# Toeplitz matrices of a long convolution: 64 rows fetched and 64 copied, or 32 rows fetched and 96 copied

## What is computed

```python
K  = _dplr_kernel(...)                                   # 64 channels x 1101 taps
Kf = jnp.fft.rfft(K, n=2 * L, axis=-1)
uf = jnp.fft.rfft(x, n=2 * L, axis=1)                    # x: (8, 1101, 64), normalized tokens
h1 = jnp.fft.irfft(uf * Kf.T[None], n=2 * L, axis=1)[:, :L, :]   # causal convolution
y1 = gelu(h1 + D * x)
y2 = gelu(y1 @ W_fc.T + b_fc) + x
y  = layernorm(y2) * ln_g + ln_b
```

## Time and profile before

| | us |
|---|---|
| median of 3 runs | 1528.23 |
| lowest and highest | 1527.93, 1532.77 |
| profiled execution | 1524.09 |
| its span, first to last instruction | 1522.4 |
| convolution loops on PE, first to last matmul | 202.1 to 299.3 |
| busy: PE, DVE, ACT, POOL | 1217.3, 827.2, 831.6, 427.0 |
| mean granted TensorE clock | 0.918 of full speed |

### The profile page before, as it was taken

How to read it: one execution, slowest core, us unless ns; L and a number is a source line. 1 busy time by engine, 2 the same in 40 slices (tenths; PEclk the granted TensorE clock), 3 DMA queues, 4 the chain that set the end, 5 groups by cost and what they waited for, 6 DMA issues and landing times.

```text
span 1522.4 us, 28792 instructions
## 1 busy us (share of the span) xinstructions
PE 1217.3 (80%) x11006; PEld 613.6 (40%) x11103; DVE 827.2 (54%) x1688; ACT 831.6 (55%) x1050; POOL 427.0 (28%) x624
## 2 busy tenths in 40 slices
PE   4894558880579988998998898899989889989942
PEld 3462357760235433433443343343344334334321
DVE  4844873357653645474575456457546554833443
ACT  0231134440245776587587667758857766876810
POOL 2000040026532123324242432423333243242321
PEclk9996779995579999999999999999999999999965
DMA  9999179704092055028008403701820560290000
GB/s 155 186 170 186 24 161 206 158 1 101 24 151 28 13 113 86 1 70 138 12 13 140 66 13 83 123 2 34 147 39 13 110 96 1 73 137 2 4 13 10
DMA packets 122173, 117.99 MB, mean 78 GB/s; under 512 B 74621, under 2 KB 91276, under 8 KB 121882
## 3 DMA queue, kind: packets, MB, share of 16 engines
q1 hardware_dynamic: 117988, 115.60, 41.8%
q10 hardware_dynamic: 3733, 0.60, 0.3%
q0 software_dynamic: 320, 0.04, 0.0%
HBM read 88.36 MB, written 22.95 MB: 73 GB/s over the span
## 4 chain that ended last, share of the span: by engine, by line
PE 38%; DVE 10%; ACT 8%; POOL 6%; issue 6%; DMA 5%; SPq 3%; POOLq 0%; DVEq 0%; ACTq 0%
PE b_pso L1974 12%; PE b_pss L1950 10%; ACT b_pb L2084 6%; POOL b_stat L2109 4%; DMA qk_parts_b<-b_qs 3%; PE b_psm L2031 3%; PE b_psm L2001 3%; DMA b_qop<-bound_part 2%; PE b_psm L2017 2%; PE b_psm L1933 2%; POOL b_pb L2128 1%; PE b_psm L2010 1%; PE b_psm L2036 1%; PE b_psm L2013 1%; SPq L1885 1%
## 5 line engine op out<-in xcount | busy, mean ns | idle before, releaser
L2084 ACT ACTIVATE b_pb<-b_pss 128x1024 f32<-128x1024 f32 (+2 forms) x736 | 661.2, 934 | 301.1 <-PE b_pss L1950 222.1
L2128 POOL TENSOR_SCALAR_AFFINE_SELECT b_pb<-b_pb 128x256 f32<-128x256 f32 (+1 forms) x544 | 224.5, 431 | 675.1 <-ACT b_pb L2084 668.8
L1974 PE MATMUL b_pso<-b_pb,b_vop 128*32 128x77 f32 (+4 forms) x5376 | 374.5, 385 | 35.2 <-POOL b_pb L2128 32.7
L1950 PE MATMUL b_pss<-b_qop,b_kop 128*128 128x512 bf16 (+3 forms) x1439 | 322.9, 331 | 32.7 <-DMA b_qop<-bound_part 12.4
L1950 PEld LDWEIGHTS b_pss<-b_qop,b_kop 128*128 128x128 bf16 x1536 | 125.7, 101 | 212.2 <-ACT b_pb L2084 96.7
L1974 PEld LDWEIGHTS b_pso<-b_pb,b_vop 128*32 128x32 f32 x5376 | 112.8, 109 | 210.8 <-issue 164.6
L2320 DVE TENSOR_TENSOR b_ofm<-b_pso,b_mk 128x512 f32<-128x512 f32 (+1 forms) x96 | 51.7, 538 | 142.9 <-PE b_pso L1974 142.1
L2109 POOL TENSOR_TENSOR b_stat<-b_stat,b_mh 128x18 f32<-128x18 f32 x34 | 108.8, 3217 | 39.5 <-DVE b_stat L2392 28.0
L919 PE MATMUL psc<-tz,ub 128*64 128x128 f32 x1152 | 79.6, 283 | 43.8 <-DVE tz L1040 35.7
L2202 DVE COPY b_ot<-b_psm 128x336 f32<-128x336 f32 (+1 forms) x96 | 40.1, 417 | 106.6 <-PE b_psm L2001 106.4
L919 PEld LDWEIGHTS psc<-tz,ub 128*64 128x64 f32 x1152 | 72.1, 142 | 51.1 <-DVE ub L1036 33.6
(11 more groups left out here) (391 smaller groups left out, 1538.0 us busy)
## 6 DMA issues: line engine op xcount, KB each, us to landing
b_qop<-qk_parts_b SPq DMA_DIRECT2D x192, 144.0 KB
tz<-taps SPq DMA_DIRECT2D x64, 304.0 KB, 9.3
x<-in_x SPq DMA_DIRECT2D x16, 1024.0 KB, 13.7
qk_parts_b<-b_qs SPq DMA_DIRECT2D x16, 864.0 KB, 5.6
b_kop<-qk_parts_b SPq DMA_DIRECT2D x192, 36.0 KB
b_mk<-b_mskf SPq DMA_DIRECT2D x128, 36.0 KB, 4.7
qk_parts_b<-b_ks SPq DMA_DIRECT2D x8, 432.0 KB, 4.0
n_late<-id_d SPq DMA_DIRECT2D x1, 2400.0 KB, 9.7
```

What stands on the lines that cost most here:

```text
L1950: mm = pe.matmul(pss[:, u % 2, b, col:col + w], lhs, qop[:, n, e, q0:q0 + w], start=True, stop=True, skip_group_check=True)
L1974: mm = pe.matmul(pso[VW * ee:VW * (ee + 1), (3 * n + x) % 2, q0 - QT * x:q0 - QT * x + w], vop[0:r, j, n, :], pb[0:r, slot_, b, cc:cc + w] ...
L2084: nc.scalar.activation(pb[:, s % PB, 0:nb, 0:w], pss[:, s % 2, 0:nb, 0:w], ACT.Exp, scale=float(HD) ** 0.5).then_inc(exped, 1)
L2128: ins = pool.affine_select(out=v_, in_=v_, compare_op=ALU.is_ge, fill=0.0, base=0, pattern=pat, channel_multiplier=-1)
```

## The change

A quarter of each matrix is fetched instead of a half. The place's "home" quarter is partitions 0, 32, 64 or 96 in turn with `k % 4`. The transfer has 32 rows of 1248 elements (4992 B a row, 156 KB). Two copies on the chip follow, both by the engine that made the one copy before. `second(k)` copies the home quarter, shifted by 32 elements, to the quarter beside it (32 partitions, 1216 elements). `other_half(k)` copies this half, shifted by 64 elements, to the other half (64 partitions, 1152 elements). The second of these reads what the first one wrote, so between them the engine waits for a semaphore that its own first copy counts: `half_a` on ACT and `dve` on DVE. A row of `tz` is 32 elements longer, the matrix sits at offset `home(k)` in it, and `taps_at` reads from there. The semaphore `warm_ok`, for which nothing waited, goes away.

```diff
+    QR = P // 4
+    home = lambda k: QR * (k % 4)
-        tz = sb("tz", [P, 2 * HC, LP + D])
+        tz = sb("tz", [P, 2 * HC, LP + 3 * QR])
+        def second(k):
+            r = home(k)
+            d = QR if r % D == 0 else -QR
+            at = QR * (r // QR % 2)
+            return tz[r + d:r + d + QR, k, at:at + LP + D], tz[r:r + QR, k, at + d:at + d + LP + D]
+        def other_half(k):
+            r = home(k)
+            s, d = (0, D) if r < D else (D, -D)
+            return tz[s + d:s + d + D, k, r:r + LP], tz[s:s + D, k, r + d:r + d + LP]
 # SP
-                        sp.dma_start(tz[0:D, k, :], bass.AP(krev_d.tensor, krev_d.offset + c0 * KREV, [[1, D], [1, LP + D]])).then_inc(s_tz[k], 16)
+                        sp.dma_start(tz[home(k):home(k) + QR, k, :], bass.AP(krev_d.tensor, krev_d.offset + c0 * KREV, [[1, QR], [1, LP + 3 * QR]])).then_inc(s_tz[k], 16)
 # PE
-                        taps_at = lambda dl: tz[:, k, LP - P - P * dl:LP - P * dl]
+                        taps_at = lambda dl: tz[:, k, home(k) + LP - P - P * dl:home(k) + LP - P * dl]
 # ACT
                 def double(k, n):
                     act.wait_ge(s_tz[k], n * 16 + 16)
-                    nc.scalar.copy(tz[D:P, k, 0:LP], tz[0:D, k, D:]).then_inc(tz_ok[k], 1)
+                    nc.scalar.copy(*second(k)).then_inc(half_a, 1)
+                    act.wait_ge(half_a, n * len(BY_ACT) + BY_ACT.index(k) + 1)
+                    nc.scalar.copy(*other_half(k)).then_inc(tz_ok[k], 1)
 # DVE
                                 v.wait_ge(s_tz[k], it * 16 + 16)
-                                cp(tz[D:P, k, 0:LP], tz[0:D, k, D:]).then_inc(tz_ok[k], 1)
-
+                                cp(*second(k)).then_inc(dve, 1)
+                                v.wait_ge(dve, it * len(BY_DVE) + BY_DVE.index(k) + 2)
+                                cp(*other_half(k)).then_inc(tz_ok[k], 1)
+
+                ch.n += NI * len(BY_DVE)
```

More of the change, by code:

```diff
@@ L877, in stage_ssm @@
         cout = [sem("conv0_copied"), sem("conv1_copied")]
-        mh_ok, ul_ok, hl_ok, warm_ok = sem("mh_ready"), sem("residual_ready"), sem("sum_ready"), sem("gelu_loaded")
+        mh_ok, ul_ok, hl_ok, half_a = sem("mh_ready"), sem("residual_ready"), sem("sum_ready"), sem("half_copied")
         wt, wb_ok, turned, y1_ok, fdone, zg, centred, squared, scaled, h_ok, h_out, prepared, psw_out = (sem(x) for x in (
@@ L955, in _ @@
                 act.wait_ge(mh_ok, 1)
-                nc.scalar.activation(warm[:], mh[:, 0:1], ACT.Gelu).then_inc(warm_ok, 1)
+                nc.scalar.activation(warm[:], mh[:, 0:1], ACT.Gelu)
                 def double(k, n):
                     act.wait_ge(s_tz[k], n * 16 + 16)
-                    nc.scalar.copy(tz[D:P, k, 0:LP], tz[0:D, k, D:]).then_inc(tz_ok[k], 1)
+                    nc.scalar.copy(*second(k)).then_inc(half_a, 1)
+                    act.wait_ge(half_a, n * len(BY_ACT) + BY_ACT.index(k) + 1)
+                    nc.scalar.copy(*other_half(k)).then_inc(tz_ok[k], 1)
                 def outputs(g, n, c0):
```

## The result

The changed kernel takes 1510.64 us (median of 20 runs) against 1525.74 us for the kernel before (20 runs): a ratio of 0.9911 with a 95% interval of 0.9892 to 0.9929, or 10.8 to 16.5 us less. The prediction, 11.2 us from 1528.2, is a ratio of 0.9927, where the two intervals meet. The range's lower end of 1511 missed the measured median by 0.4 us; the kernel before had itself moved, from 1528.2 in 3 runs to 1525.7 in 20.

What follows compares the result with a forecast made beforehand. Transfers were taken to bound the convolution at 12 us an iteration, with ACT next at 9.48. 69.6 - 56.4 - 1.7 = 11.5 us, taken as 11.2, gave 1528.2 - 11.2 = 1517.0 us, range 1511 to 1524.

Steps and rivals of the forecast that it cites:

- The transfer, 0.77 us: Tap load in the convolution: 0.51 of the bytes at the old rate, so 0.77 us for 1.50, 6.2 an iteration.
- the sum: Forecast total: 69.6 us before, 56.4 after from iteration 2 on, less 1.7 for a late start; gain 11.5, taken as 11.2.
- The fixed part of a landing: Part of a tap transfer's issue-to-landing time beyond its pitch: 3.8 - 1.5, about 2.3 us.
- the ring: Ring of one place: signal, transfer, two ACT copies and convolution, in all 6.9 of 9.5 us, so it has room.
- the cover of 2.6 us: Slack in the ring of one place; if gone (landing of 5 us, not 3.1), about 6 us come back over the stage.
- The copies and their waits: Two copies per matrix: 1.21 and 1.15 us on ACT, 0.79 and 0.75 on DVE, with 0.03 us for each wait.
- The iteration: Steady 8 channels: ACT 9.48 us, DVE 8.84, PE 8.72, transfers 6.2; ACT becomes the bound, for 12.0 before.
- The beginning: POOL's instructions block DVE's copies; iteration 1 begins 3.2 us later, gives back 1.5, so iteration 2 is 1.7 late.
- The walk: Order of work at the beginning retraced with L1005 at 202, 204 and 206; the end moved by -0.3 to +1.2 us.
- 1: Rival: fewer rows don't shorten the transfer, which stays at 1.5 us; about 1531.5 us, up to 1535; chance of slower 0.06.
- 2: Rival: ACT's waits or `second` copies cost more; 0.2 us more on both gives 1520.5; chance 0.12 mild, 0.07 strong.
- 3: Rival: more gain, as L1005's block meets no waiting work or `second` copies are shorter; PE bounds, 1513 us; chance 0.07.

Runs made afterwards that it cites:

- e3: Changed kernel with every home quarter at partition 0 and 64 rows fetched instead of 32; ratio to the kernel before 1.0046, stage 184.6 us.
- e5: Kernel before, with POOL's copy to `ul` and addition into `hh` waiting for the last convolution; ratio to the kernel before 0.9979, stage 177.4 us.
- e2: Changed kernel with every home quarter at partition 0 and 48 rows fetched instead of 32; ratio to the kernel before 1.0029, stage 184.3 us.
- e6: As e3, but with the home quarter at partition 32, so the 64 rows land in partitions 32 to 95; ratio to the kernel before 0.9920.
- e8: Changed kernel with two matrices fetched whole and not copied, four left to DVE and two to ACT; ratio to the kernel before 0.9869, stage 161.1 us.
- e11: As e9, plus a 128 x 1 addition on POOL at the stage's start; ratio to the kernel before 0.9846, 1499.13 us beside 1514.65 for the changed kernel.
- e4: Changed kernel with POOL's copy to `ul` and addition into `hh` waiting for the last convolution; ratio to the kernel before 0.9828, stage 153.8 us.
- e1: Changed kernel with all quarters fetched to partitions 0 to 31, not four places in turn; ratio to the kernel before 0.9929, stage 166.8 us.
- e10: Kernel before, one copy per matrix, with fetched halves landing below and above partition 64 in turn; ratio to the kernel before 0.9933, stage 170.9 us.
- e9: e8 and e4 together: two matrices fetched whole and POOL's two long instructions late; ratio to the kernel before 0.9836, stage 151.0 us.

## Why the prediction was right

- **What bounds the kernel before: the transfers.** Right. e3 brought them back and lost all of the gain, and in e5 the kernel before did not get faster without DVE's stalls.
- **The transfer, 0.77 us.** Right as a number, 0.74 to 0.77 with the engines full, and wrong as a step, so the number was luck. "0.51 of the bytes" is not why it got shorter: 0.77 of the bytes (e2) gave no time back, and all of them (e6) took 1.0 to 1.1 us and cost the kernel nothing. Where the rows land decides. The port rule of the Trainium skill, which the prediction set beside the sum, fits e2 and e3 and in the main e6. For 32 rows at one place bytes and rows on a port both give a half, so the sum did not notice. Whether the loads of 16 partitions follow the same rule no run shows.
- **The fixed part of a landing, 3.8 - 1.5 = 2.3 us.** Wrong: the whole landing of a quarter takes 2.3 at least. It did no harm, as the ring had more room than I gave it. (By the prediction's own terms the cover of 2.6 us is gone at a landing of 5.7, not 5; a landing took 2.6.)
- **The copies and their waits.** Right: 1.205 and 1.151 us on ACT (1.21 and 1.15 in the sum), 0.786 and 0.755 on DVE (0.79 and 0.75), 0.02 to 0.04 us between them. 32 partitions took no less time than 64.
- **The iteration: ACT 9.48, DVE 8.84, PE 8.72.** Measured 9.28, 8.90, and 8.74 for PE in e8. The ranking is right: PE waited for ACT, 0.34 us an iteration, and DVE ran ahead. ACT's is 0.2 too long, since a copy of results starts up to 0.1 us before the end of the copy in front of it (234.17 against 233.11 + 1.15), where I had counted a gap of 0.03, and takes 1.05 or 1.06 us for 1.08.
- **The beginning.** Right in its course: the first matmul 0.8 us later against POOL's copy (0.8 by the terms predicted), PE's stop behind channel 5, two channels left for after the stall. Mis-sized in one term: a channel at the low clock (1.2 GHz instead of 2.4) takes 216.59 - 214.40 = 2.19 us at a granted clock of 0.50, twice 1.09, not 1.78. That is less even than the 2.15 beside it, which holds 17 of a channel's 20 instructions, and rows 6 show 204.30 - 202.14 = 2.16 between channels. DVE was also caught in the first copy for channel 6 and not behind it (it ends at 213.55, 0.65 behind POOL), and the first channel of iteration 1 still took 1.68 us for 1.15. Against that, the sum's own subtraction was 0.2 too small: 10.4 - 8.7 gives back 1.7, not 1.5. Together iteration 2 began 40.5 us behind POOL's first copy (227.98 - 187.52), where the prediction has 38.9.
- **The sum.** From POOL's first copy to the last matmul's start: 95.0 us predicted (287.8 for its end, so 287.5 - 192.5) and 94.9 measured (282.4 - 187.5). The two slips, 1.6 late in the beginning and 1.7 early in the iterations (1.0 of it 5 x 0.2), cancel. That the total came out so close is luck; the mechanism did not depend on it.
- **L1005's wait of 7 us.** The walk allowed for an earlier start with fewer bytes under way. It did not: 6.94 us with the DMA engines at a share of 0.07 (196.00 to 202.90), 7.23 with them full (1.05 in 201.00 to 208.10 of the kernel before). e11 shows it to be a cost of POOL's first addition, wherever that stands. POOL has no other addition ahead of it in the program.
- **Rivals.** 1 fell, and e2 shows how near it was: at partitions 0 to 47 it would have been right. 2 fell with the rows of ACT above. 3 fell too: DVE's copy did stand beside L1005, and 32 partitions took no less than 64. It took e4's edit to be free of the first. The DMA share was forecast as 0.65 and is 0.52, since a transfer that meets no queue shows 0.6 us of busy time (0.52 x 9.28 / 8) and not 0.77.

## What to carry to other kernels

Before a load is cut to save bytes, ask which partitions its rows land in: the same 64 rows cost 1.56 us at partition 0 and 1.0 to 1.1 at partition 32. When a full queue is relieved, go through the stalls that it used to hide; here the POOL block was worth 0.1 us of the stage before the change and 12 us after it, more than the change itself. And when a blocking instruction is moved, look up what stands at its new place, small instructions too.

## What the runs showed of the hardware

- Rows of a load count by where they land: 32 rows at partitions 0 to 31 took 0.77 us (e1), 48 rows at 0 to 47 1.57 us (e2), 64 rows at 0 to 63 1.56 us (e3), and 64 rows at 32 to 95 1.0 to 1.1 us (e6).
- Loads that go to the two halves of the partitions in turn moved 231 GB/s, against 207 for one half alone (e10). The Trainium skill, SBUF — State Buffer, section "Can I just issue two DMAs to hit both halves?", gives 6% for such a pair; here it is 12%, and the measurement decides.
- POOL's first addition begins 6.9 to 7.7 us late, with a memset or a copy in front of it and the DMA engines busy or not. The second begins at once (278.20, behind a copy that ended at 278.12). The Trainium skill, GPSIMD Engine Reference, section "2.1 Instruction dispatch", states about 6 us for a load of code at the first call to a freshly loaded kernel; the runs show a wait of about that size, and not that it is code.
- An addition on POOL held up a DVE instruction with two inputs in SBUF too: four products of 128 x 16 elements took 10.21 us in e11 and 0.41 in e9.
- Between executions of unchanged stages, the front stage varied by 7.4 us and the attention stage by 10. Why was not looked into.
